# Linear attention as one pipeline over units of two tile pairs, with its weights built in an earlier stage

## The chip, the cores and the metric

The kernel runs on one core of one Trainium2 chip. The metric is the device time of the whole program in microseconds, as the median over several runs. The kernel is one program of about 4.3 ms in which nine stages follow each other; the change is inside one of them and touches one other.

## The reference, cut to what matters

The input X has 2 x 1024 rows of 128 values. Two local stacks of six layers each make up most of the time; between them stands a linear attention over the pairs of rows (0, n) and (1, n), so the sequence has two positions:

```python
qn = _ln(query, g1, b1)                    # query = layernorm(x)
q = relu(_phm(qn, qA, qS, qb))
k = relu(_phm(query, kA, kS, kb))
v = _phm(query, vA, vS, vb)
idx = np.pi / 2 * jnp.arange(1, L + 1)[None, :, None] / L      # L = 2 positions, 16 heads of 8
q_, k_ = concat([q * s, q * c]), concat([k * s, k * c])        # s, c = sin(idx), cos(idx)
attn = (q_ @ (k_.T @ v)) / max(q_ . sum(k_), 1e-6)
out = _ln(attn + qn, g2, b2)
x = x + _phm(out, oA, oS, ob) + out
```

`_phm(x, A, S, b)` is x @ W + b, where the 128x128 matrix W is a sum of four Kronecker products of a 4x4 with a 32x32 matrix.

## The kernel before

X lies in SBUF as 16 tiles of 128 rows by 128 columns; `NT` is 16, `TB` is 8 tiles of each position, and `NG` is 4 groups of four tiles. PS is the PSUM memory of eight banks of 512 columns. The names of the engines in the code are `te` (TensorE, PE in the profile), `ve` (VectorE, DVE), `ac` (ScalarE, ACT), `gp` (GpSimd, POOL) and `sp` (SyncE). The order on each engine is the order in which the code writes it; no scheduler changes it. Engines wait for each other's semaphores. `then` makes VectorE wait for its own last instruction, and `fence()` is a barrier of all engines that also clears the semaphores.

`linear_attention` has three passes with a barrier behind each. The first builds the four weights on VectorE (L1124, L1126), and then, group by group, takes statistics (L201, L205, L208), lets POOL take the root (L212), normalises on VectorE (L221), turns on TensorE (L237), copies on ScalarE (L1098), multiplies by the weights of K and V (L1115), and adds the bias on VectorE out of PSUM (L1105, L1138). The second does the same for Q with gain and shift (L227, L229), and behind its last group VectorE alone does the attention for all tiles (`dve_attend`, L1174 to L1188). The third normalises the result, multiplies by the last weight (L1205) and adds to X (L1216 to L1219). Statistics of the next group run ahead, but the wait on `kv_mm`, `lq_mm` or `lo_mm` stands in VectorE's order before the next group's normalisation:

```python
if g < NG - 1:
    norm_stats(g + 1, X)
norm_apply(g, X, group(XN, g))
ve.wait_ge(kv_mm, g + 1)
```

In `cope_attention`, an earlier stage of the same form, POOL only takes the roots of four groups and adds a bias behind the next barrier (L1055).

## Time and profile before

| what | us |
|---|---|
| median of 3 runs | 4346.16 (4344.17 to 4351.9) |
| the profiled execution | 4355.26, of which the span is 4354.0 |
| linear attention, from first to last instruction of VectorE | 2488.55 to 2634.38 |
| first local stack | 778.83 to 2487.48 |
| second local stack, with the output's transfer | 2635.45 to 4353.9 |

The rows of the profile are of one execution. Busy times are the sums of an engine's instructions in a stretch. The granted clock is a share of TensorE's full 2.4 GHz, so 0.50 is 1.2 GHz. A tensor multiplication in f32 appears as two matmul records of PE.

### The profile page before, as it was taken

The page shows a single profiled execution, that of the slowest core. Times are in us where ns is not written, and L with a number is a line of the kernel's source. Part 1 is how long each engine was busy: PE and PEld are TensorE (multiplying, and loading weights), DVE is VectorE, ACT ScalarE, POOL GpSimd, SP SyncE. Part 2 cuts the span into 40 slices and gives each one's busy share as a digit, 9 for nine tenths or more (in the row PEclk, how much of TensorE's full clock was granted, in tenths as well). Part 3 has the DMA queues.
Part 4 walks back from the last instruction along what each step waited for, and adds up shares of the span by engine and source line. Part 5 has one row for each costly group of instructions (what it writes and reads, how often), then busy time and mean ns, then how long its engine had stood idle before and what let it go on. Part 6 is the DMA issues. An engine that isn't in the chain of part 4 may idle for free. (4 is left out here: it accounts for less than half of the span.)

```text
span 4354.0 us, 158762 instructions
## 1 busy us (share of the span) xinstructions
PE 3861.5 (89%) x66864; PEld 2706.7 (62%) x66864; DVE 3055.7 (70%) x6301; ACT 2565.4 (59%) x4921; POOL 2642.3 (61%) x2220
## 2 busy tenths in 40 slices
PE   7988792799999999999999536999999999999996
PEld 5655561466666766667666424666666676666764
DVE  4456576777777778777787357778777777877773
ACT  3335360466767666666676304666666666766764
POOL 2039092676676767667676206766666677767772
PEclk7569896899999999999999757999999999999998
DMA  3000000132333323333333101333333233333222
GB/s 97 1 1 1 1 1 0 43 95 65 93 80 77 88 72 87 82 82 82 77 86 84 38 0 41 87 76 86 78 84 80 74 88 84 78 80 80 67 71 55
DMA packets 303234, 276.83 MB, mean 64 GB/s; under 512 B 158136, under 2 KB 201664, under 8 KB 302528
## 3 DMA queue, kind: packets, MB, share of 16 engines
q1 hardware_dynamic: 302528, 266.68, 24.1%
q8 instruction: 533, 8.73, 0.9%
q14 instruction: 173, 1.42, 0.1%
HBM read 51.58 MB, written 1.05 MB: 12 GB/s over the span
## 5 line engine op out<-in xcount | busy, mean ns | idle before, releaser
L1350 PE MATMUL PS<-l_wqkv,XNT 128*128 128x512 f32 x768 | 392.1, 633 | 0.6 <-issue 0.4
L1344 PE MATMUL PS<-l_wqkv,XNT 128*128 128x512 f32 x768 | 381.1, 619 | 2.5 <-issue 1.5
L1337 PE MATMUL PS<-l_wqkv,XNT 128*128 128x512 f32 x768 | 368.8, 603 | 6.1 <-DVE l_UQ L1619 2.3
L1492 ACT ACTIVATE m_sq<-PS 128x512 f32<-128x512 f32 x384 | 225.9, 595 | 197.4 <-PE PS L1344 160.6
L1492 ACT ACTIVATE l_sq<-PS 128x512 f32<-128x512 f32 x384 | 226.0, 595 | 197.3 <-PE PS L1344 160.4
L1758 POOL TENSOR_TENSOR l_Pm<-l_Pm,l_rs 128x1024 f32<-128x1024 f32 x96 | 182.8, 1904 | 237.1 <-DVE l_rs L1629 237.1
L1758 POOL TENSOR_TENSOR m_Pm<-m_Pm,m_rs 128x1024 f32<-128x1024 f32 x96 | 182.8, 1904 | 233.2 <-DVE m_rs L1629 233.2
L1647 DVE TENSOR_TENSOR XN<-PS,XN 128x128 f32<-128x128 f32 x192 | 56.1, 292 | 281.4 <-PE PS L1396 281.4
L1616 DVE TENSOR_TENSOR l_QR<-PS,l_rot 128x512 f32<-128x512 f32 x192 | 131.7, 686 | 164.8 <-ACT l_sq L1492 158.5
L1616 DVE TENSOR_TENSOR m_QR<-PS,l_rot 128x512 f32<-128x512 f32 x192 | 131.7, 686 | 164.2 <-ACT m_sq L1492 158.0
L1753 POOL TENSOR_TENSOR m_QR<-m_QR,m_UQ 128x1024 f32<-128x1024 f32 x96 | 227.7, 2372 | 19.8 <-DVE m_UQ L1619 19.8
L1753 POOL TENSOR_TENSOR l_QR<-l_QR,l_UQ 128x1024 f32<-128x1024 f32 x96 | 227.7, 2372 | 19.5 <-DVE l_UQ L1619 19.5
L212 POOL TENSOR_TENSOR rstd<-rstd,minus_half 128x4 f32<-128x4 f32 x40 | 41.7, 1044 | 307.2 <-DVE rstd L208 307.2
L1753 POOL TENSOR_TENSOR m_KR<-m_KR,m_UK 128x1024 f32<-128x1024 f32 x96 | 226.8, 2363 | 0.2 <-DVE m_UK L1619 0.2
L1753 POOL TENSOR_TENSOR l_KR<-l_KR,l_UK 128x1024 f32<-128x1024 f32 x96 | 226.7, 2362 | 0.2 <-DVE l_UK L1619 0.2
L1634 DVE TENSOR_REDUCE l_sums<-l_sq 128x16 f32<-128x1024 f32 x192 | 219.1, 1182 | 0.0
L1634 DVE TENSOR_REDUCE m_sums<-m_sq 128x16 f32<-128x1024 f32 x192 | 219.1, 1182 | 0.0
L1366 PEld LDWEIGHTS PS<-m_V,m_pT 64*32 64x32 f32 x12288 | 131.6, 106 | 126.6 <-issue 66.5
L1366 PEld LDWEIGHTS PS<-l_V,l_pT 64*32 64x32 f32 x12288 | 132.2, 106 | 123.2 <-issue 70.8
L1350 PEld LDWEIGHTS PS<-l_wqkv,XNT 128*128 128x128 f32 x768 | 133.5, 194 | 116.8 <-issue 100.0
L1344 PEld LDWEIGHTS PS<-l_wqkv,XNT 128*128 128x128 f32 x768 | 130.9, 190 | 115.6 <-issue 96.1
L1366 PE MATMUL PS<-m_V,m_pT 64*32 64x64 f32 x12288 | 153.1, 227 | 49.4 <-DMA m_V<-m_Vt 35.5
(363 smaller groups left out, 11342.7 us busy)
## 6 DMA issues: line engine op xcount, KB each, us to landing
l_V<-l_Vt SPq DMA_DIRECT2D x576, 128.0 KB
m_V<-m_Vt SPq DMA_DIRECT2D x576, 128.0 KB
l_V<-l_Vt SPq DMA_DIRECT2D x384, 64.0 KB
m_V<-m_Vt SPq DMA_DIRECT2D x384, 64.0 KB
l_wqkv<-l_wqkv_dram SPq DMA_DIRECT2D x144, 128.0 KB, 2.4
l_rot<-l_rot_dram SPq DMA_DIRECT2D x48, 256.0 KB, 3.9
l_wo<-l_wo_dram SPq DMA_DIRECT2D x24, 256.0 KB, 3.5
l_w<-l_w_dram SPq DMA_DIRECT2D x12, 341.0 KB
```

What stands on the lines that cost most here:

```text
L212: gp.tensor_tensor(rstd[:, g % 2, :], rstd[:, g % 2, :], minus_half[:, 0:4], ALU.pow).then_inc(rstd_out)
L1337: te.matmul(PS[:, b, :], tile_T(n), weights(n, b * 512, (b + 1) * 512), start=True, stop=True).then_inc(q_pr)
L1344: te.matmul(PS[:, 2 + b, :], tile_T(n), weights(n, INNER + b * 512, INNER + (b + 1) * 512), start=True, stop=True).then_inc(k_pr)
L1350: m = te.matmul(PS[:, r, :], tile_T(n), wv, start=True, stop=True)
L1366: m = te.matmul(PS[LW * w:LW * (w + 1), 6 + r, c * LD:(c + 1) * LD], pT[64 * r:64 * r + 64, c, LW * w:LW * (w + 1)], V2[64 * r:64 * r + 64 ...
L1492: ac.activation(sq[:, c, b * 512:(b + 1) * 512], PS[:, 2 * c + b, :], ACT.Square).then_inc(sq_out)
L1616: ve.tensor_tensor(R[:, n % 2, heads, :], src, over(rot[:, par, 2 * c, i, :], 1, [P, 8, LD]), ALU.mult)
L1634: ve.tensor_reduce(sums2[:, c * LH:(c + 1) * LH, 0], sq[:, c, :].rearrange("p (h d) -> p h d", d=LD), AX, ALU.add).then_inc(ssr_out)
L1647: ve.tensor_tensor(Y[:, i, :], PS[:, 5, 0:D], Y[:, i, :], ALU.add).then_inc(y_add)
L1753: gp.tensor_tensor(R[:, n % 2, :, :], R[:, n % 2, :, :], U[:, :, :], ALU.add).then_inc((aq_out, ak_out)[c])
L1758: gp.tensor_tensor(pm, pm, over(rs[:, :], 2, [P, 16, 2 * LW]), ALU.mult).then_inc(pn_out)
```

## The change

The weights of the linear attention are built on POOL in the cope stage, behind its four roots, and kept in `d_w`. `linear_attention` is written anew. A unit `u` is two tiles of position 0 and the same two of position 1 (`tile`), so that a unit has all that its attention needs. In each of seven rounds every engine does what is due for different units: in round r keys, values and queries of unit r, attention of unit r - 1, second norm of unit r - 2, output of unit r - 3. There is one barrier, at the end. Statistics of all 16 tiles are taken at once; the norm of the norm is not measured but computed from the first variance (`root2`). ScalarE normalises (activation with scale and bias) and takes K, Q and V out of PSUM; TensorE adds the bias by a product of a row of ones with the bias row into the same bank (`projected`); POOL adds shifts and gains and sums the normalised result into X. What is removed are the three passes printed above. The diff, with declarations left out:

```diff
@@ -98,7 +98,7 @@
-        d_fact, d_blocks = sb("d_fact", P, 4, 4, 4), sb("d_blocks", P, 4, 4, D // 4)
+        d_w = sb("d_w", P, 4, D)
...
+        d_fact, d_blocks, d_part = se("d_fact", P, 4, 4, 4), se("d_blocks", P, 4, 4, D // 4), se("d_part", P, 2, D)
@@ -1021,6 +1022,16 @@
                 def pool():
                     for g in range(NG):
                         norm_root(g)
+                    shape = [P, 4, D // 4]
+                    for m4 in range(4):
+                        whole = d_w[:, m4, :].rearrange("p (j l) -> p j l", j=4)
+                        for k in range(4):
+                            to = whole if k == 0 else d_part[:, k % 2, :].rearrange("p (j l) -> p j l", j=4)
+                            G.step(gp.tensor_tensor(to, over(d_fact[:, m4, k, :], 2, shape), over(d_blocks[:, m4, k, :], 1, shape), ALU.mult))
+                            G.wait()
+                            if k:
+                                G.step(gp.tensor_tensor(whole, whole, to, ALU.add))
+                                G.wait()
@@ -1068,160 +1079,233 @@
...
         def linear_attention():
...
+                wq, wk, wv, wo = (d_w[:, m4, :] for m4 in range(4))
                 g1, b1, g2, b2 = (d_gain[:, k, :] for k in range(4))
...
+                U = [P, NG, 4, D]
+                xn, qn, k4, v4, q4 = (sl(n, *U) for n in ("xn", "QN", "k", "v", "q"))
...
+                xT, qT, aT = (sl(n, P, 4 * P) for n in ("xT", "qT", "aT"))
...
+                def tile(u, j):
+                    return TB * (j // 2) + 2 * u + j % 2
+                def unit(src, u):
+                    return src[:, :, :].rearrange("p (s i) d -> p s i d", s=2)[:, :, 2 * u:2 * u + 2, :]
...
+                def pe():
+                    def turned(bank, src):
                         for j in range(4):
+                            m = te.transpose(PS[:, bank, j * P:(j + 1) * P], src[:, j, :], ident[:, :])
+                        return m
+                    def projected(bank, m4, lhs, w):
+                        te.matmul(PS[:, bank, :], ones[0:1, :], over(d_bias[0:1, m4, :], 1, [1, 4, D]), start=True, stop=False, skip_group_check=True)
                         for j in range(4):
+                            m = te.matmul(PS[:, bank, j * D:(j + 1) * D], lhs[:, j * P:(j + 1) * P], w, start=False, stop=True, skip_group_check=True)
+                        return m
+                    te.wait_ge(dready, 1)
+                    for r in range(NG + 3):
+                        if r < NG:
+                            te.wait_ge(dxn_out, r + 1)
+                            if r:
+                                te.wait_ge(dxT_out, r)
+                            turned(0, xn[:, r, :, :]).then_inc(dxT_mm)
+                            te.wait_ge(dxT_out, r + 1)
+                            if r:
+                                te.wait_ge(dk_out, r)
+                                te.wait_ge(dv_out, r)
+                            projected(1, 1, xT, wk)
+                            projected(2, 2, xT, wv).then_inc(dkv_mm)
+                            te.wait_ge(dqn_out, r + 1)
+                            if r:
+                                te.wait_ge(dqT_out, r)
+                            turned(3, qn[:, r, :, :]).then_inc(dqT_mm)
+                            te.wait_ge(dqT_out, r + 1)
+                            if r:
+                                te.wait_ge(dq_out, r)
+                            projected(4, 0, qT, wq).then_inc(dq_mm)
+                        u = r - 3
+                        if u >= 0:
+                            te.wait_ge(daff_out, u + 1)
+                            if u:
+                                te.wait_ge(daT_out, u)
+                            turned(5, an[:, u, :, :]).then_inc(daT_mm)
+                            te.wait_ge(daT_out, u + 1)
+                            if u:
+                                te.wait_ge(dx_out, u)
+                            projected(6, 3, aT, wo).then_inc(do_mm)
+                def act():
+                    for r in range(NG + 3):
+                        if r < NG:
+                            ac.wait_ge(dshift_out, 1)
+                            for j in range(4):
+                                n = tile(r, j)
+                                m = ac.activation(xn[:, r, j, :], X[:, n, :], ACT.Identity, scale=root[:, n:n + 1], bias=shift[:, n:n + 1])
+                            m.then_inc(dxn_out)
+                            ac.wait_ge(dxT_mm, r + 1)
+                            if r:
+                                ac.wait_ge(dkv_mm, r)
+                            ac.copy(xT[:, :], PS[:, 0, :]).then_inc(dxT_out)
+                            ac.wait_ge(dkv_mm, r + 1)
+                            ac.activation(k4[:, r, :, :].rearrange("p j d -> p (j d)"), PS[:, 1, :], ACT.Relu).then_inc(dk_out)
+                            ac.copy(v4[:, r, :, :].rearrange("p j d -> p (j d)"), PS[:, 2, :]).then_inc(dv_out)
+                            ac.wait_ge(dqT_mm, r + 1)
+                            if r:
+                                ac.wait_ge(dq_mm, r)
+                            ac.copy(qT[:, :], PS[:, 3, :]).then_inc(dqT_out)
+                            ac.wait_ge(dq_mm, r + 1)
+                            ac.activation(q4[:, r, :, :].rearrange("p j d -> p (j d)"), PS[:, 4, :], ACT.Relu).then_inc(dq_out)
+                        u = r - 2
+                        if 0 <= u < NG:
+                            ac.wait_ge(dashift_out, u + 1)
+                            for j in range(4):
+                                m = ac.activation(an[:, u, j, :], att[:, u, j, :], ACT.Identity, scale=aroot[:, u % 2, j:j + 1], bias=ashift[:, u % 2, j:j + 1])
+                            m.then_inc(dan_out)
+                        u = r - 3
+                        if u >= 0:
+                            ac.wait_ge(daT_mm, u + 1)
+                            if u:
+                                ac.wait_ge(do_mm, u)
+                            ac.copy(aT[:, :], PS[:, 5, :]).then_inc(daT_out)
+                def dve():
+                    def attend(u):
+                        ve.wait_ge(dk_out, u + 1)
+                        ve.wait_ge(dv_out, u + 1)
+                        ve.wait_ge(dq_out, u + 1)
+                        V.wait()
+                        for s in range(2):
+                            q = q4[:, u, 2 * s:2 * s + 2, :].rearrange("p i d -> p (i d)")
+                            m = ve.tensor_tensor(prod[:, s, :, :], k4[:, u, :, :].rearrange("p (k i) d -> p k (i d)", k=2), over(q, 1, [P, 2, 2 * D]), ALU.mult)
+                        then(m)
+                        then(ve.tensor_reduce(dots[:, :, :, :].rearrange("p s k h -> p (s k h)"),
+                                              prod[:, :, :, :].rearrange("p s k (h d) -> p (s k h) d", d=DH), AX, ALU.add))
+                        then(ve.tensor_tensor(dots[:, :, :, :], dots[:, :, :, :], turn[:, :, :, 0:2, :].rearrange("p s k i h -> p s k (i h)"), ALU.mult))
+                        then(ve.tensor_tensor(den[:, :, :], dots[:, :, 0, :], dots[:, :, 1, :], ALU.add))
+                        then(ve.tensor_scalar(den[:, :, :], den[:, :, :], 1e-6, None, ALU.max))
+                        then(ve.reciprocal(den[:, :, :], den[:, :, :]))
+                        then(ve.tensor_tensor(dots[:, :, :, :], dots[:, :, :, :], over(den[:, :, :], 2, [P, 2, 2, 2 * H]), ALU.mult))
+                        for s in range(2):
+                            weight = over(dots[:, s, :, :].rearrange("p k h -> p (k h)"), 2, [P, 4 * H, DH])
+                            m = ve.tensor_tensor(prod[:, s, :, :].rearrange("p k (h d) -> p (k h) d", d=DH),
+                                                 v4[:, u, :, :].rearrange("p j (h d) -> p (j h) d", d=DH), weight, ALU.mult)
+                        then(m)
+                        a = att[:, u, :, :].rearrange("p (s i) d -> p s (i d)", s=2)
+                        then(ve.tensor_tensor(a, prod[:, :, 0, :], prod[:, :, 1, :], ALU.add))
+                        then(ve.tensor_tensor(att[:, u, :, :], att[:, u, :, :], qn[:, u, :, :], ALU.add))
+                    def measure(u):
+                        par = u % 2
+                        if u >= 2:
+                            ve.wait_ge(dan_out, u - 1)
+                        for j in range(4):
+                            m = ve.bn_stats(ast[:, par, j, :], att[:, u, j, :])
+                        then(m)
+                        for j in range(4):
+                            m = ve.bn_aggr(amv[:, par, j, :], ast[:, par, j, :])
+                        then(m)
+                        ve.tensor_scalar(aroot[:, par, :], amv[:, par, :, 1], EPS, None, ALU.add).then_inc(davar_out)
+                    for n in range(NT):
+                        m = ve.bn_stats(st[:, n, :], X[:, n, :])
+                    then(m)
+                    for n in range(NT):
+                        m = ve.bn_aggr(mv[:, n, :], st[:, n, :])
+                    then(m)
+                    ve.tensor_scalar(root[:, :], mv[:, :, 1], EPS, None, ALU.add).then_inc(dvar_out)
+                    ve.wait_ge(droot_out, 1)
+                    ve.scalar_tensor_tensor(shift[:, :], mv[:, :, 0], -1.0, root[:, :], ALU.mult, ALU.mult).then_inc(dshift_out)
+                    then(ve.tensor_tensor(root2[:, :], mv[:, :, 1], root[:, :], ALU.mult))
+                    then(ve.tensor_tensor(root2[:, :], root2[:, :], root[:, :], ALU.mult))
+                    ve.tensor_scalar(root2[:, :], root2[:, :], EPS, None, ALU.add).then_inc(dvar2_out)
+                    ve.wait_ge(droot2_out, 1)
+                    ve.wait_ge(dready, 1)
+                    for r in range(NG + 4):
+                        if r < NG:
+                            ve.wait_ge(dxn_out, r + 1)
+                            for j in range(4):
+                                n = tile(r, j)
+                                m = ve.scalar_tensor_tensor(qn[:, r, j, :], xn[:, r, j, :], root2[:, n:n + 1], g1, ALU.mult, ALU.mult)
+                            m.then_inc(dqg_out)
+                        u = r - 2
+                        if 0 <= u < NG:
+                            ve.wait_ge(daroot_out, u + 1)
+                            ve.scalar_tensor_tensor(ashift[:, u % 2, :], amv[:, u % 2, :, 0], -1.0, aroot[:, u % 2, :], ALU.mult, ALU.mult).then_inc(dashift_out)
+                        u = r - 1
+                        if 0 <= u < NG:
+                            attend(u)
+                            measure(u)
+                        u = r - 4
+                        if u >= 0:
+                            ve.wait_ge(do_mm, u + 1)
+                            ve.wait_ge(dres_out, u + 1)
+                            ve.tensor_tensor(unit(X, u), PS[:, 6, :].rearrange("p (s i d) -> p s i d", s=2, i=2), unit(X, u), ALU.add).then_inc(dx_out)
+                def pool():
...
+                    G.wait()
+                    gp.memset(ones[:, :], 1.0).then_inc(dready)
+                    gp.wait_ge(dvar_out, 1)
+                    gp.tensor_tensor(root[:, :], root[:, :], minus_half[:, 0:NT], ALU.pow).then_inc(droot_out)
+                    gp.wait_ge(dvar2_out, 1)
+                    gp.tensor_tensor(root2[:, :], root2[:, :], minus_half[:, 0:NT], ALU.pow).then_inc(droot2_out)
+                    for r in range(NG + 3):
+                        if r < NG:
+                            gp.wait_ge(dqg_out, r + 1)
+                            gp.tensor_tensor(qn[:, r, :, :], qn[:, r, :, :], over(b1, 1, [P, 4, D]), ALU.add).then_inc(dqn_out)
+                        u = r - 2
+                        if 0 <= u < NG:
+                            gp.wait_ge(dan_out, u + 1)
+                            G.step(gp.tensor_tensor(an[:, u, :, :], an[:, u, :, :], over(g2, 1, [P, 4, D]), ALU.mult))
+                            G.wait()
+                            gp.tensor_tensor(an[:, u, :, :], an[:, u, :, :], over(b2, 1, [P, 4, D]), ALU.add).then_inc(daff_out)
+                            gp.wait_ge(daff_out, u + 1)
+                            gp.tensor_tensor(unit(X, u), unit(X, u), pairs(an[:, u, :, :]), ALU.add).then_inc(dres_out)
+                        u = r - 1
+                        if 0 <= u < NG:
+                            gp.wait_ge(davar_out, u + 1)
+                            gp.tensor_tensor(aroot[:, u % 2, :], aroot[:, u % 2, :], minus_half[:, 0:4], ALU.pow).then_inc(daroot_out)
+                pe()
+                act()
+                dve()
+                pool()
                 fence()
```

The order on the engines follows. On TensorE, where the names before the arrow are the target bank and behind it weights and moving data, the stage began with a turn and key and value products and had these rows at the start of the first and the second pass:

```order
L237 MATMUL PS<-ident,XN 128x128 x4
L1115 MATMUL PS<-d_wk,xT 128x128
L1115 MATMUL PS<-d_wv,xT 128x128
...
L237 MATMUL PS<-ident,d_QN 128x128 x4
L1153 MATMUL PS<-d_wq,xT 128x128 x4
```

It now has this in round 3, the first in which all parts are present:

```order
L1128 MATMUL PS<-ident,d_xn 128x128 x4
L1132 MATMUL PS<-d_bias,d_ones 128x512
L1134 MATMUL PS<-d_w,d_xT 128x128 x4
L1132 MATMUL PS<-d_bias,d_ones 128x512
L1134 MATMUL PS<-d_w,d_xT 128x128 x4
L1128 MATMUL PS<-ident,d_QN 128x128 x4
L1132 MATMUL PS<-d_bias,d_ones 128x512
L1134 MATMUL PS<-d_w,d_qT 128x128 x4
L1128 MATMUL PS<-ident,d_an 128x128 x4
L1132 MATMUL PS<-d_bias,d_ones 128x512
L1134 MATMUL PS<-d_w,d_aT 128x128 x4
```

Keys, values, queries and output of different units now stand behind each other, each with a bias product of 512 columns ahead of it.

On ScalarE the whole stage was twelve copies between the last layer before and the table load of the next stack:

```order
L1547 ACTIVATE xT<-PS,l_b 128x512 x2
L1547 ACTIVATE xT<-PS,l_b 85x512
L1098 COPY xT<-PS 128x512 x12
L1549 ACT_TABLE_LOAD
L1526 COPY XNT<-PS 64x512
```

Now rounds 2 and 3 read so on ScalarE:

```order
L1175 ACTIVATE d_xn<-X,d_shift,d_root 128x128 x4
L1180 COPY d_xT<-PS 128x512
L1182 ACTIVATE d_k<-PS 128x512
L1183 COPY d_v<-PS 128x512
L1187 COPY d_qT<-PS 128x512
L1189 ACTIVATE d_q<-PS 128x512
L1194 ACTIVATE d_an<-d_att,d_ashift,d_aroot 128x128 x4
L1175 ACTIVATE d_xn<-X,d_shift,d_root 128x128 x4
L1180 COPY d_xT<-PS 128x512
```

The normalisation of the next round stands behind the last evacuation of this one and, from round 2 on, behind that of a result.

On POOL the stage had four roots in each pass, with the barriers (L120) between:

```order
L120 ISA
L212 TENSOR_TENSOR rstd<-rstd,minus_half 128x4 x4
L120 ISA
L212 TENSOR_TENSOR rstd<-rstd,minus_half 128x4 x4
L120 ISA
```

Now, from the stage's begin to its first sum into X:

```order
L1281 MEMSET d_turn 128x128 x4
L1283 MEMSET d_ones 128x128
L1285 TENSOR_TENSOR d_root<-d_root,minus_half 128x16
L1287 TENSOR_TENSOR d_root<-d_root,minus_half 128x16
L1291 TENSOR_TENSOR d_QN<-d_QN,d_gain 128x512 x2
L1303 TENSOR_TENSOR d_aroot<-d_aroot,minus_half 128x4
L1291 TENSOR_TENSOR d_QN<-d_QN,d_gain 128x512
L1295 TENSOR_TENSOR d_an<-d_an,d_gain 128x512
L1297 TENSOR_TENSOR d_an<-d_an,d_gain 128x512
L1299 TENSOR_TENSOR X<-X,d_an 128x2x256
L1303 TENSOR_TENSOR d_aroot<-d_aroot,minus_half 128x4
```

Behind the three operations of a unit (L1295, L1297, L1299) stands the root of the unit after it (L1303).

## Rows read from the trace of the kernel before

**Rows 1.** The page, its head.
```profile
span 4354.0 us, 158762 instructions
```

**Rows 2.** Order of time on VectorE: start, length, instruction, idle before it and its releaser.
```profile
2488.55 0.29 DVE L1124 TENSOR_TENSOR d_wq<-d_fact,d_blocks 128x128 f32<-128x128 f32 x1 [1.07 <-PEq L120]
...
2497.68 0.87 DVE L201 BATCH_NORM_STATS2 stats<-X 128x6 f32<-128x128 f32 x4
...
2633.69 0.69 DVE L1219 TENSOR_TENSOR X<-PS,X 128x512 f32<-128x512 f32 x1 [2.58 <-PE PS L1205]
2635.45 0.87 DVE L201 BATCH_NORM_STATS2 stats<-X 128x6 f32<-128x128 f32 x4 [1.06 <-PEq L120]
```

**Rows 3.** Stretches: PE, PEld, DVE, ACT, POOL busy (count), clock, DMA share, GB/s.
```profile
2538.21:2599.88 61.67, 12.77 (x48) 9.99 (x48) 43.11 (x93) 2.34 (x4) 4.17 (x4) 0.51 0.00 0
...
2488.55:2635.45 146.90, 45.13 (x176) 36.80 (x176) 91.05 (x257) 7.06 (x13) 12.55 (x13) 0.51 0.00 0
```

**Rows 4.** Order of time on all engines: the first group's keys and values.
```profile
2501.64 1.12 PE L237 MATMUL PS<-ident,XN 128*128 128x128 f32 x4 [15.61 <-DVE XN L221]
2502.80 0.58 ACT L1098 COPY xT<-PS 128x512 f32<-128x512 f32 x1 [20.55 <-PE PS L237]
...
2503.43 0.80 PE L1115 MATMUL PS<-d_wk,xT 128*128 128x128 f32 x2 [0.68 <-ACT xT L1098]
...
2506.58 0.63 PE L1115 MATMUL PS<-d_wv,xT 128*128 128x128 f32 x2
2507.26 0.69 DVE L1105 TENSOR_TENSOR d_kv<-PS,d_bias 128x512 f32<-128x512 f32 x1 [5.67 <-PE PS L1115]
```

**Rows 5.** Groups of instructions in the stage: count, busy us, mean ns, idle before.
```profile
L1176 DVE TENSOR_REDUCE d_dots<-d_prod 128x128 f32<-128x1024 f32 x4 | 4.9, 1220 | 0.1
...
L205 DVE BATCH_NORM_AGGREGATE meanvar<-stats 128x2 f32<-128x6 f32 x48 | 4.5, 157 | 0.4
...
L201 DVE BATCH_NORM_STATS2 stats<-X 128x6 f32<-128x128 f32 x16 | 3.5, 277 | 0.0
...
L1216 DVE TENSOR_TENSOR X<-X,xn 128x512 f32<-128x512 f32 x4 | 2.8, 691 | 0.1
...
L1180 DVE RECIPROCAL d_den<-d_den 128x256 f32<-128x256 f32 x1 | 1.8, 1753 | 0.0
```

**Rows 6.** Groups on POOL by form, 665 to 830 us.
```profile
L212 POOL TENSOR_TENSOR rstd<-rstd,minus_half 128x4 f32<-128x4 f32 x8 | 8.3, 1044 | 27.9 <-DVE rstd L208 27.9
...
L1055 POOL TENSOR_TENSOR X<-X,c_bo 128x512 f32<-128x512 f32 x4 | 4.9, 1266 | 65.3 <-SPq L120 65.3
...
L748 POOL TENSOR_TENSOR X<-X,g_y 128x128 f32<-128x128 f32 x2 | 0.9, 452 | 0.2
```

**Rows 7.** Order of time on ScalarE: normalising four tiles by scale and bias.
```profile
2470.97 1.65 ACT L1533 ACTIVATE xn<-l_xsh,l_fmid,l_frs 128x128 f32<-128x128 f32 x4 [16.94 <-DVE l_fmid L1667]
```

**Rows 8.** Order of time on TensorE, second stack's begin: two 512-column products.
```profile
2655.50 1.96 PE L1337 MATMUL PS<-l_wqkv,XNT 128*128 128x512 f32 x4 [2.21 <-DVE m_UQ L1619]
```

**Rows 9.** Order of time on TensorE in the cope stage.
```profile
679.53 5.49 PE L953 MATMUL PS<-c_w,xT 128*128 128x384 f32 x8 [0.68 <-ACT xT L961]
689.29 1.12 PE L237 MATMUL PS<-ident,xn 128*128 128x128 f32 x4 [4.28 <-DVE xn L221]
```

**Rows 10.** Stretches, columns as in rows 3.
```profile
685.00:687.00 2.00, 0.01 (x1) 0.00 (x0) 1.95 (x3) 0.00 (x0) 0.00 (x0) 0.84 0.00 0
689.00:691.00 2.00, 1.12 (x4) 0.72 (x4) 0.23 (x1) 0.56 (x1) 0.33 (x1) 0.51 0.00 0
...
2654.00:2656.50 2.50, 1.00 (x3) 0.55 (x4) 2.50 (x7) 0.00 (x0) 1.07 (x1) 1.00 0.00 0
...
80.00:240.00 160.00, 159.33 (x1154) 104.88 (x1153) 64.64 (x95) 55.61 (x95) 13.19 (x9) 0.50 0.00 1
```

**Rows 11.** One line of VectorE in the mixture stage: min, median, max ns.
```profile
L707 DVE TENSOR_TENSOR g_y<-g_y,g_x x16: 1225/1562/3390, 544.2 to 665.7; 128x1024 f32<-128x1024 f32 x16
```

More of the change, by code:

```diff
@@ L1091, in then @@
                     V.wait()
-                def turn_copies(mm):
-                    for g in range(NG):
-                        ac.wait_ge(turn_mm, g + 1)
-                        if g >= 2:
-                            ac.wait_ge(mm, g - 1)
-                        ac.copy(xT4[:, g % 2, :], PS[:, 7 * (g % 2), :]).then_inc(xT_out)
-                def roots():
-                    for g in range(NG):
-                        norm_root(g)
-                def biased(to, bank_cols, bias, out_sem):
-                    ve.tensor_tensor(to, bank_cols, over(bias, 1, [P, 4, D]), ALU.add).then_inc(out_sem)
@@ L1156, in dve_queries @@
-                def dve_queries():
-                    norm_stats(0, XN)
-                    for g in range(NG):
-                        if g < NG - 1:
-                            norm_stats(g + 1, XN)
-                        norm_apply(g, XN, group(QN, g), affine=(g1, b1))
-                        ve.wait_ge(lq_mm, g + 1)
-                        biased(group(q, g), PS[:, 1:5, 0:D], bs["q"][:, :], lq_out)
-                        ve.wait_ge(lq_out, g + 1)
-                        V.step(ve.tensor_scalar(group(q, g), group(q, g), 0.0, None, ALU.max))
@@ L1178, in dve_attend @@
-                    then(ve.tensor_tensor(den[:, :, :], dots[:, :, 0, :], dots[:, :, 1, :], ALU.add))
-                    then(ve.tensor_scalar(den[:, :, :], den[:, :, :], 1e-6, None, ALU.max))
-                    then(ve.reciprocal(den[:, :, :], den[:, :, :]))
-                    then(ve.tensor_tensor(dots[:, :, :, :], dots[:, :, :, :], over(den[:, :, :], 2, [P, 2, 2, P]), ALU.mult))
-                    for s in range(2):
-                        for k, to in ((0, prod), (1, prod2)):
-                            a = over(heads(dots[:, s, k, :]), 3, full)
-                            m = ve.tensor_tensor(split(to[:, :, :]), split(kv[:, TB * k:TB * (k + 1), D:]), a, ALU.mult)
-                        then(m)
-                        then(ve.tensor_tensor(prod[:, :, :], prod[:, :, :], prod2[:, :, :], ALU.add))
-                        then(ve.tensor_tensor(att[:, TB * s:TB * (s + 1), :], prod[:, :, :], QN[:, TB * s:TB * (s + 1), :], ALU.add))
@@ L1208, in dve_out @@
-                def dve_out():
-                    norm_stats(0, att)
-                    for g in range(NG):
-                        par, xg = g % 2, group(X, g)
-                        if g < NG - 1:
-                            norm_stats(g + 1, att)
-                        norm_apply(g, att, xn4[:, par, :, :], affine=(g2, b2))
-                        ve.wait_ge(xn_out, g + 1)
-                        then(ve.tensor_tensor(xg, xg, xn4[:, par, :, :], ALU.add))
-                        then(ve.tensor_tensor(xg, xg, over(bs["o"][:, :], 1, [P, 4, D]), ALU.add))
-                        ve.wait_ge(lo_mm, g + 1)
-                        ve.tensor_tensor(xg, PS[:, 1 + par, :].rearrange("p (j d) -> p j d", j=4), xg, ALU.add).then_inc(lo_out)
```

100 lines of the change are left out of this document (18 added, 82 removed).

## The prediction

> **What bounds the kernel now.** I read the page first (its span [rows 1]), then the stretches of the linear attention, then the order of time on VectorE, on TensorE and on ScalarE there. The stage lasts from VectorE's first weight product at 2488.55 to the first statistics of the next stack at 2635.45 [rows 2], 146.9 us of 4354.0. Nothing of another stage runs inside it: a barrier stands at both ends and two stand within. In these 146.9 us VectorE works 91.1, TensorE 45.1, POOL 12.6, ScalarE 7.1, and TensorE's granted clock is 0.51, the lower of its two levels of 1.2 and 2.4 GHz [rows 3]. The reader is to see that no engine is full. The engines work one after another, as one group of keys and values shows: VectorE normalises, TensorE turns (1.12), ScalarE copies (0.58), TensorE multiplies (2503.43 to 2507.2), and VectorE, which has waited 5.67 us, takes the result out [rows 4]. In the stretch that holds the query pass and the attention VectorE is busy 43.1 of 61.7 [rows 3]. So the stage is a chain, and its length is the sum of VectorE's work and of what VectorE waits for.
>
> **What the change removes.** The 28 weight products and sums leave VectorE; between the row at 2488.55 and the first statistics at 2497.68 they fill 9.1 us, 28 at 0.326 [rows 2]. Two barriers go, each 1.1 us as the idle time before the row at 2635.45 shows [rows 2]. Statistics of the second norm go, since it is now computed from the first. What remains is a new order of work, so I don't subtract: I build the new stage's length from its chain and set it against 146.9.
>
> **Head.** Sixteen statistics at 4 in 0.87 are 3.5 us, sixteen aggregations at 94 ns are 1.5, one scalar and the handoffs 0.3: 5.3 [rows 5]. Then POOL takes a power of 16 columns. The trace has only 4 columns, at 1.04 [rows 6]. Bounds: 1.0 if the cost is fixed, 4.2 if it is all by column. Plain POOL work grows with its elements (128 columns 0.45, 512 columns 1.27, [rows 6]), so about 0.2 is fixed and 4 columns of power cost 0.8: I take 3.4. With the shift, 0.3, the first normalisation on ScalarE starts at 9.0. The second power is beside ScalarE's and TensorE's first work and costs nothing here; it has some 4 us of cover before TensorE asks for the query's norm.
>
> **A round.** In each of four rounds ScalarE and TensorE hand one unit to and fro, and neither has another unit to work on: ScalarE's next normalisation stands behind its last copy of this round. The steps, with handoffs: normalise, 4 in 1.65 [rows 7]; turn, 1.15 at the low clock as in [rows 4], 0.65 at the high one; copy 0.65; keys and values; their two evacuations 1.25 (TensorE turns the queries beside them); copy 0.65; query product; evacuation 0.65. A 128-column product costs 0.427 at the low clock (eight in 3.8 less 0.35 of latency, [rows 4]), so the new 512-column bias product costs 1.71, as much as four of them: the bias is no longer added on VectorE but doubles TensorE's work. Keys and values are 2 x 1.71 + 8 x 0.427 + 0.35 = 7.2 low; the high clock halves all but the latency, 3.8, and two 512-column products in 1.96 at the high clock agree with that [rows 8]. The query product is 3.8 or 2.1. A round is 17.0 at the low clock and 11.4 at the high one. From the third round on ScalarE also normalises an attention result, 1.7.
>
> **Which clock.** In the cope stage a stretch of 5.49 us from 679.53 brought the clock up as it ended (0.84 between 685 and 687), and an idle of 4.28 us behind it lost it again, 0.51 between 689 and 691 [rows 9, 10]. An idle of 2.21 us in the next stack did not lose it (1.00, [rows 8, 10]). Here keys and values run 7.2 us at the low clock, longer than that stretch, so it rises within them; I take it after 4.5 us, and the product ends at 5.9. That makes round 0 14.0. Between the query product and the next turn lie 0.65 + 1.65 = 2.3 us, close to the gap that kept it: rounds 1 and 2 get 11.9, the high value with 0.5 for a partial loss. With ScalarE's extra 1.7 the gap is 4.0, close to the one that lost it, so round 3 starts low, 14.0. Round 3 begins at 9.0 + 14.0 + 11.9 + 11.9 + 1.7 = 48.5.
>
> **Tail**, counted from there. POOL gives unit 0 its gain, its shift and its sum into X, three 128x512 operations at 1.27 to 1.3 [rows 6] (3.9), and only behind them in its order stands unit 1's root (1.1); VectorE's shift for unit 1 follows at 5.2. Attend for unit 2: two products 1.3, reduction 1.26, five operations of 64 or 128 columns 1.7, of which I put the reciprocal of 64 columns at 0.55 (1.75 for 256, [rows 5]), two weightings 1.3, two sums 1.4 (512 columns in 0.69, [rows 5]), in all 7.0 and 0.1 for handoffs, 7.1; statistics 1.5. ScalarE's last copy of round 3 is at 14.0, unit 1's normalisation ends at 15.7, POOL's three operations at 19.6, the root of unit 2 at 20.7, the shift at 20.9. Here VectorE waits for POOL. Attend for unit 3 with what POOL costs it (next paragraph), 9.6, ends at 30.5, its statistics at 32.0, the sum of unit 0 into X, 0.7, at 32.7. Behind that sum TensorE can do the outputs of units 1, 2 and 3: product 3.0, then twice turn, copy and product 4.5 (5.6 low, 3.4 high, I take the middle), 44.7, last sum 45.4. The stage is 48.5 + 45.4 + barrier 1.1 = 95.0 against 146.9: 51.9 saved.
>
> **POOL beside VectorE.** A VectorE sum of 1,024 columns whose operands both lie in SBUF takes 1.22 at least and up to 3.39 in the mixture stage, where POOL is busy; the median of 16 is 1.57 [rows 11]. Six of Attend's operations have such operands, and POOL's three for unit 2 fall into Attend for unit 3. Bounds: nothing, or all of POOL's 3.8; I take 2.5, and 0.8 in Attend for unit 2, which is off the chain. The Trainium skill, "SBUF — State Buffer", Who interferes with whom, says that such a VectorE instruction and a POOL instruction that reads SBUF contend, and that the second blocks wholly until the first ends; by that rule the term is 3.8 and the time 1.3 us more. It speaks against handing POOL this work, and the trace agrees with the direction.
>
> **Weights in the cope stage.** POOL's last root there is over before VectorE's attention begins, and it then idles 65.3 us until the sums of L1055 [rows 6]. The 28 operations at 0.45 are 12.6 us and fit. Cost 0; if VectorE had to give way for all of them, 12.6.
>
> **The rivals.** (a) As summed, own range 4287 to 4301, 0.50. (b) The clock falls in every round, because the turns at a round's start don't hold it: rounds 1 and 2 cost 14.0, +4.2, 4298; 0.15. For it: the cope stage's turns at 689.29 ran low [rows 9]; against it the 2.21 us gap. The Trainium skill, "TensorE: Matmul & The Clock Gate", Part 4, says that a transpose doesn't count as busy work for the clock in the way a product does; by it the turns here would hold nothing and the time is 4298, where the sum has 4294. (c) The clock stays low throughout as before: 9.0 + 3 x 17.0 + 1.7, tail 51.4 by the same steps, 114.2 with the barrier, 32.7 saved, 4313; 0.08. Against it: a stretch of 7.2 us is longer than any that the stage has now. (d) High throughout: 85.7, 61.2 saved, 4285; 0.15. (e) VectorE gives way to the weights in the cope stage: 4294 + 12.6 = 4307; 0.05. (f) Slower: the next stack, on which TensorE is nearly full, meets the state of 80 to 240 us, where TensorE was busy 159.3 of 160 and yet got 0.50 [rows 10]. Each us of its work then takes two, so 104 us at the low clock eat the 52 saved, and a hold of 160 us gives +80, 4374. Nothing in the diff touches that stack; 0.05. (g) The gain is eaten by something unseen and nothing changes, 4346; 0.02.
>
> **How the numbers follow.** The profiled run took 4355.3, its span 4354.0; 4355.3 - 51.9 = 4303.4. It lay 9.1 above the median of the runs, 4346.2, so the forecast for the median is 4294. The range reaches down to (d) with a power of 1.0 (2.4 less), 4283, and a little contention less, 4281; upward past (b) and (e) towards (c), to 4309, which leaves out about half of (c) and the slow cases, together some 0.15. About 0.2%, 8.7 us, is what a measurement of this kernel can tell from no change. Faster 0.93, same 0.02, slower 0.05.
>
> **What would show it.** One barrier pair around a stage of about 94 us with no idle between passes; sixteen-column powers on POOL of 3 to 4 us; keys and values in about 6 us, then under 4; VectorE waiting for POOL's root before Attend of units 2 and 3; 28 POOL operations in the cope stage and no longer VectorE rows there. I am wrong if ScalarE stalls between units (its order shows no table load there), if the clock never rises, or if Attend is much over 8 us.

## The result and the profile after

The changed kernel takes 4313.73 us (median of 4 runs, 4304.96 to 4314.31). The kernel before took 4345.16 on the same chip. The ratio is 0.9923, interval [0.9908, 0.9938]: 31.4 us are saved where 52 were forecast, and the median lies above the forecast range of 4281 to 4309. The profiled execution took 4313.86, its span 4312.6.

The stage, in VectorE's order of time in the changed kernel, from its first to the first row of the next stack; between them the two waits to look at:

```profile
2492.85 3.19 DVE L1242 BATCH_NORM_STATS2 d_st<-X 128x6 f32<-128x128 f32 x16 [1.18 <-PEq L121]
...
2578.36 0.16 DVE L1265 SCALAR_TENSOR_TENSOR d_ashift<-d_amv,d_aroot 128x4 f32<-128x4 f32 x1 [9.59 <-POOL d_aroot L1303]
...
2594.32 0.69 DVE L1274 TENSOR_TENSOR X<-PS,X 128x512 f32<-128x512 f32 x1 [3.54 <-PE PS L1134]
...
2603.25 0.87 DVE L202 BATCH_NORM_STATS2 stats<-X 128x6 f32<-128x128 f32 x4 [1.18 <-PEq L121]
```

It lasts 110.4 us against the 146.9 of [rows 2, 3] and the 95.0 of the sum. The same kernel by stretches, columns as in [rows 3]: the stage, then its head, its three first rounds and the rest, the cope stage, and the second stack.

```profile
2492.85:2603.25 110.40, 70.16 (x208) 41.88 (x208) 50.76 (x145) 25.72 (x57) 32.91 (x28) 0.55 0.00 0
...
2492.85:2500.68 7.83, 0.00 (x0) 0.00 (x0) 4.74 (x35) 0.01 (x1) 3.71 (x6) 0.53 0.00 1
2500.68:2516.70 16.02, 12.23 (x38) 7.28 (x38) 1.53 (x7) 4.28 (x9) 4.16 (x2) 0.59 0.00 1
2516.70:2534.52 17.82, 14.13 (x38) 8.29 (x38) 9.21 (x25) 4.28 (x11) 3.27 (x2) 0.51 0.00 0
2534.52:2553.88 19.36, 14.13 (x38) 8.30 (x38) 9.29 (x26) 5.82 (x15) 2.32 (x1) 0.50 0.00 0
2553.88:2603.25 49.37, 29.67 (x94) 18.00 (x94) 25.98 (x53) 11.34 (x27) 19.45 (x17) 0.57 0.00 0
...
672.59:781.66 109.07, 36.38 (x96) 22.75 (x96) 63.67 (x103) 7.26 (x12) 20.92 (x37) 0.56 0.00 0
...
2603.25:4312.60 1709.35, 1606.12 (x31584) 1131.97 (x31584) 1266.62 (x2528) 1132.68 (x2112) 1160.13 (x984) 0.98 0.30 77
```

The same two stretches of the kernel before, not shown until now:

```profile
673.76:778.83 105.07, 33.32 (x96) 19.71 (x96) 62.94 (x104) 7.26 (x12) 9.17 (x9) 0.60 0.00 0
...
2635.45:4354.00 1718.55, 1610.60 (x31584) 1134.45 (x31584) 1263.99 (x2528) 1133.82 (x2112) 1159.98 (x984) 0.98 0.30 77
```

The spans differ by 41.4: 36.5 is the stage; 9.2 is the second stack, which has the same instructions and was merely longer in that execution of before; the cope stage gives back 4.0; the start and the first stack make up the rest. Whole executions scatter by about 10 us in this way, so the stage's length in the traces says more about the change than one total does.

The stage is 15.4 us longer than the sum, and 13.7 of this lie in the first three rounds. The head is 7.8 (forecast 9.0), the three rounds 53.2 (14.0 + 11.9 + 13.6 = 39.5), the rest with its barrier 49.4 (46.5). Round 3, with which the rest begins, missed in the same way: ScalarE's last evacuation in it ended 17.9 us after its begin, where the forecast had 14.0. In rounds 1 and 2 TensorE is busy 14.1 of 17.8 and 19.4 at a clock of 0.51 and 0.50. The first round and the begin of the next in order of time on TensorE, in the changed kernel:

```profile
2504.23 2.07 PE L1132 MATMUL PS<-d_bias,d_ones 1*128 1x512 f32 x2 [0.67 <-ACT d_xT L1180]
2506.23 2.08 PE L1134 MATMUL PS<-d_w,d_xT 128*128 128x128 f32 x8
2508.23 2.07 PE L1132 MATMUL PS<-d_bias,d_ones 1*128 1x512 f32 x2
2510.23 2.08 PE L1134 MATMUL PS<-d_w,d_xT 128*128 128x128 f32 x8
...
2513.96 1.12 PE L1132 MATMUL PS<-d_bias,d_ones 1*128 1x512 f32 x2 [0.80 <-ACT d_qT L1187]
...
2518.39 1.11 PE L1128 MATMUL PS<-ident,d_xn 128*128 128x128 f32 x4 [2.22 <-ACT d_xn L1175]
```

Three things are to be seen. Keys and values run 7.87 us without a gap, and the last product (2.08) is as slow as the first: the clock has not risen within them, only behind them, ahead of the query's bias (1.12); the granted clock is 0.50 up to 2513.1 and 1.00 from 2514 on. It is 0.50 again from 2517.4 on, within the pause of 2.22 us, and the next turn is slow (1.11). And a product begins 2.00 us behind the one before it, where four 128-column products should take 1.71.

### The profile page after: what moved, and what is told of

Its sections match the earlier page's. It is cut to its first block and busy times, and to the rows that moved or that the text cites. A ratio compares the mean times of both kernels' runs of the same rounds, so it can differ in the third digit from the quotient of the medians.

```text
span 4312.6 us, 158783 instructions
## 1 busy us (share of the span) xinstructions
PE 3882.3 (90%) x66896; PEld 2713.4 (63%) x66896; DVE 3020.3 (70%) x6190; ACT 2583.8 (60%) x4965; POOL 2674.5 (62%) x2263
## 3 DMA queue, kind: packets, MB, share of 16 engines
HBM read 51.58 MB, written 1.05 MB: 12 GB/s over the span
## 5 line engine op out<-in xcount | busy, mean ns | idle before, releaser
L1434 PEld LDWEIGHTS PS<-l_wqkv,XNT 128*128 128x128 f32 x768 | 132.3, 192 | 114.8 <-issue 98.0
L1428 PEld LDWEIGHTS PS<-l_wqkv,XNT 128*128 128x128 f32 x768 | 131.0, 190 | 114.7 <-issue 95.1
L1421 PEld LDWEIGHTS PS<-l_wqkv,XNT 128*128 128x128 f32 x768 | 132.8, 193 | 102.1 <-issue 102.1
L1450 PE MATMUL PS<-l_V,l_pT 64*32 64x64 f32 x12288 | 153.8, 228 | 45.1 <-DMA l_V<-l_Vt 31.4
```

The costliest lines, as they stand in the source:

```text
L1421: te.matmul(PS[:, b, :], tile_T(n), weights(n, b * 512, (b + 1) * 512), start=True, stop=True).then_inc(q_pr)
L1428: te.matmul(PS[:, 2 + b, :], tile_T(n), weights(n, INNER + b * 512, INNER + (b + 1) * 512), start=True, stop=True).then_inc(k_pr)
L1434: m = te.matmul(PS[:, r, :], tile_T(n), wv, start=True, stop=True)
L1450: m = te.matmul(PS[LW * w:LW * (w + 1), 6 + r, c * LD:(c + 1) * LD], pT[64 * r:64 * r + 64, c, LW * w:LW * (w + 1)], V2[64 * r:64 * r + 64 ...
```

## The experiments

In all of them the stage is measured as above, from VectorE's first statistics to those of the next stack, in the one execution of each kernel that was profiled. The ratio intervals of the change, e2 and e3 overlap, and so do those of e1, e5, e6 and e7: within these two groups the totals can't tell the kernels apart, and what is said of them goes by the stage.

| kernel | median, us | before, same chip | ratio, interval | stage, us |
|---|---|---|---|---|
| the change | 4313.73 | 4345.16 | 0.9923 [0.9908, 0.9938] | 110.40 |
| e1_rows128 | 4297.87 | 4354.24 | 0.9868 [0.9852, 0.9884] | 97.09 |
| e2_rows32 | 4319.01 | 4354.24 | 0.9917 [0.9903, 0.9932] | 106.77 |
| e3_rows64 | 4319.75 | 4354.24 | 0.9918 [0.9901, 0.9934] | 113.75 |
| e4_nobias | 4290.3 | 4354.24 | 0.985 [0.9835, 0.9865] | 81.72 |
| e5_early | 4307.77 | 4363.73 | 0.9871 [0.9844, 0.9897] | 90.00 |
| e6_rows128_early | 4302.16 | 4363.73 | 0.9848 [0.9823, 0.9874] | 83.47 |
| e7_rows128_tail | 4309.26 | 4363.73 | 0.987 [0.9843, 0.9897] | 94.04 |
| e8_weights_only | 4349.36 | 4363.73 | 0.9969 [0.9953, 0.9986] | 137.53 |
| b1_all | 4290.97 | 4357.21 | 0.9843 [0.9825, 0.9861] | 77.74 |
| b2_root_first | 4290.02 | 4357.21 | 0.9851 [0.9825, 0.9876] | 77.19 |

**e1_rows128.** The bias product gets 128 rows of weights 1/128 (the bias tile already holds the bias in every row). The result, the columns and the number of instructions stay.

```diff
-te.matmul(PS[:, bank, :], ones[0:1, :], over(d_bias[0:1, m4, :], 1, [1, 4, D]), ...)
+te.matmul(PS[:, bank, :], ones[0:128, :], over(d_bias[0:128, m4, :], 1, [128, 4, D]), ...)
-gp.memset(ones[:, :], 1.0)
+gp.memset(ones[:, :], 1.0 / 128)
```

> The bias product uses all 128 rows (weights of 1/128, the bias row repeated on all partitions) in place of one row; its 512 columns stay. Theory A, the clock takes a product that uses one row for almost no activity: now the clock rises within the keys-and-values stretch of every round, the stage falls from 110.4 us to 92 to 98, and the 0.29 us that each change between one-row and full products costs (28 changes, 8 us, inside this figure) are gone. Theory B, the pauses of 2 us and more between the rounds hold the clock down whatever the product: granted clock stays at 0.50 to 0.55 and the stage only loses the changes, 102 to 106 us. Median of the runs: A 4293 to 4300, B about 4306.

The same rows of TensorE in this kernel:

```profile
2503.89 2.08 PE L1132 MATMUL PS<-d_bias,d_ones 128*128 128x512 f32 x2 [0.68 <-ACT d_xT L1180]
2505.76 1.92 PE L1134 MATMUL PS<-d_w,d_xT 128*128 128x128 f32 x8
2507.47 1.91 PE L1132 MATMUL PS<-d_bias,d_ones 128*128 128x512 f32 x2
2509.18 1.29 PE L1134 MATMUL PS<-d_w,d_xT 128*128 128x128 f32 x8
2510.30 0.60 PE L1128 MATMUL PS<-ident,d_QN 128*128 128x128 f32 x4
...
2516.36 1.05 PE L1128 MATMUL PS<-ident,d_xn 128*128 128x128 f32 x4 [2.23 <-ACT d_xn L1175]
```

The clock now rises within keys and values, as the prediction had it, in this and in each later round, and the products follow each other at 1.71. ScalarE's normalisations stand at 2500.33, 2514.67, 2528.60 and 2543.97: rounds of 14.3, 13.9 and 15.4 where the changed kernel has 16.0, 17.8 and 19.4. The stage is 97.1, where the prediction's sum had 95.0. What still fails is the pause: the granted clock is 1.00 through its 2.23 us and falls as the next turn begins, which takes 1.05. Ahead of round 3 it outlasts even 3.78 us and the turn (0.66), and falls as keys and values begin:

```profile
2545.67 0.66 PE L1128 MATMUL PS<-ident,d_xn 128*128 128x128 f32 x4 [3.78 <-ACT d_xn L1175]
2547.01 1.93 PE L1132 MATMUL PS<-d_bias,d_ones 128*128 128x512 f32 x2 [0.68 <-ACT d_xT L1180]
```

**e2_rows32 and e3_rows64.** The same edit with 32 rows of 1/32 and with 64 rows of 1/64.

> The bias product uses 32 rows (weights 1/32). Theory A with activity by rows used: too little, clock low as with one row, stage 108 to 112 us. Theory B: the same stage as with one row. If the clock rises here as with 128 rows, it is not the count of rows but something of the single row.

> The bias product uses 64 rows (weights 1/64). Theory A by rows used: between the two, the clock rises in some of the rounds, stage 95 to 110 us. Theory B: no difference from one row, 110 us.

With 64 rows, on TensorE:

```profile
2505.74 2.07 PE L1132 MATMUL PS<-d_bias,d_ones 64*128 64x512 f32 x2 [0.68 <-ACT d_xT L1180]
2507.74 2.07 PE L1134 MATMUL PS<-d_w,d_xT 128*128 128x128 f32 x8
2509.74 2.07 PE L1132 MATMUL PS<-d_bias,d_ones 64*128 64x512 f32 x2
2511.74 2.08 PE L1134 MATMUL PS<-d_w,d_xT 128*128 128x128 f32 x8
```

Neither the late clock nor the 2.00 us is gone; both come as with one row. With 1, 32 and 64 rows the clock rose within keys and values in none of the twelve rounds; with 128 it did in all eight of e1 and e7. In the 64-row kernel the pause ahead of round 1 did not cost the clock, which fell only behind the turn:

```profile
2519.91 0.66 PE L1128 MATMUL PS<-ident,d_xn 128*128 128x128 f32 x4 [2.23 <-ACT d_xn L1175]
```

Both stages miss what was expected, e2 by 1.2 us below 108 to 112 and e3 by 3.8 us above 95 to 110. The stages of 106.8, 110.4 and 113.8 with 32, 1 and 64 rows are not in the order of the rows; they differ by where the clock happened to rise for a while. Among the row counts tried only the full 128 behaves otherwise. Whether the clock answers to the rows or to the 0.29 us that TensorE loses at each change of rows no run tells apart, since the two came and went together.

**e4_nobias.** It leaves the biases out of the four projections, so its output lacks them.

> Leaves the sixteen bias products out, so K, Q, V and the output lack their biases; all else as in the changed kernel. It prices what adding the bias on TensorE costs. TensorE's keys and values are then eight products, 3.8 us at the low clock, 8.0 before; the queries 2.1 in place of 4.3. Both theories: a round falls from 17.8 to about 11.5, the stage to 78 to 84 us. Theory A also says that full products with no weak ones between may bring the clock up in some rounds; theory B says it stays at 0.50.

```profile
2494.02:2575.74 81.72, 38.28 (x176) 32.61 (x176) 51.78 (x146) 25.84 (x57) 32.97 (x28) 0.60 0.00 1
```

TensorE is busy 38.3 us instead of 70.2, and the stage is 28.7 us shorter: that is the whole price of the bias products where they stand in the changed kernel. The clock stays at 0.60 in the mean, hardly above the 0.55 with them; e1, with as many columns as the changed kernel, has 0.72. All products here have 128 rows, and yet the query products of rounds 0 and 3 still run at the low clock (2.08 us each): full rows alone don't bring it up.

**e5_early and e6_rows128_early.** ScalarE normalises the next unit right behind its copy of xT, while TensorE multiplies keys and values; e5 with one row, e6 with 128.

```diff
 ac.copy(xT[:, :], PS[:, 0, :]).then_inc(dxT_out)
+if r + 1 < NG:
+    normal(r + 1)        # the four activations that stood at the head of round r + 1
 ac.wait_ge(dkv_mm, r + 1)
```

> One-row bias products as in the changed kernel; ScalarE normalises the next unit right behind its copy of this one, while TensorE multiplies, and no longer behind the last evacuation. The pause of TensorE before a turn falls from 2.2 us to about 0.6. The gap theory (the pauses hold the clock down) expects the clock to rise now: stage 95 us or less. The row theory expects it to stay at 0.50 apart from chance rises, and the stage to lose only 3 x 1.65 us of the chain: 104 to 107 us.

> Both: 128-row bias products and the early normalisation. Row theory: the clock rises in the first round and, with pauses of 0.6 us, is kept through the rounds, so a round is at most 10 to 11 us and VectorE's 11 us of a unit become the limit: stage 82 to 88 us. If the pauses did not matter for keeping it, only 5 us come off the 97.1 of the 128-row kernel: 92 us.

On TensorE in e5, from the first query product on:

```profile
2519.88 1.12 PE L1132 MATMUL PS<-d_bias,d_ones 1*128 1x512 f32 x2 [0.80 <-ACT d_qT L1192]
2520.93 1.16 PE L1134 MATMUL PS<-d_w,d_qT 128*128 128x128 f32 x8
2521.93 0.60 PE L1128 MATMUL PS<-ident,d_xn 128*128 128x128 f32 x4
...
2525.39 1.22 PE L1132 MATMUL PS<-d_bias,d_ones 1*128 1x512 f32 x2
2526.54 2.07 PE L1134 MATMUL PS<-d_w,d_xT 128*128 128x128 f32 x8
```

Without the pause the clock passes from round 0 into round 1 (0.60 for the turn). Then it falls, and the product at 2526.54 takes 2.07, in the midst of gapless keys and values, one-row products among them. So with one-row products the clock neither comes up in time nor stays. But the stage of 90.00 is what the gap theory expected (95 or less) and far below the 104 to 107 of the row theory: the mean clock of the stage is 0.67 where the changed kernel has 0.55, and taking out the pauses alone gave more (20.4 us) than filling the rows alone (13.3). Both matter here. With 128 rows and no pause it holds; in e6:

```profile
2525.00:2552.00 27.00, 19.54 (x110) 13.86 (x110) 22.10 (x51) 12.17 (x27) 6.69 (x6) 1.00 0.00 0
```

The stage of e6 is 13.6 us shorter than that of e1, and that of e5 20.4 shorter than the changed kernel's. The edit also takes 1.65 us of normalising and the handoffs out of rounds 1 to 3, some 5 us, so these sums aren't the clock's alone.

**e7_rows128_tail.** e1 with VectorE's sum of unit r-4 into X ahead of the attention of unit r-1.

> The 128-row kernel with VectorE's sum into X of unit r - 4 written ahead of the attention of unit r - 1 instead of behind it, so that the output product of unit 1 need not wait 13.5 us for the attention of unit 3. If the tail is TensorE's row of three output products behind that sum, the stage loses 2 to 5 us of 97.1. If the tail is the way of unit 3 itself (root, shift, normalisation, POOL's gain and shift, turn, product), it loses under 1 us.

94.04 against 97.09. In the changed kernel the bias product for the output of unit 1 waits for that sum until 2590.24, 11.46 us; the tail is held up by an order of two VectorE steps. By the totals e7 and e1 can't be told apart.

**e8_weights_only.** The kernel before with nothing but the weights moved to POOL in the cope stage.

> The kernel before with one part of the change alone: the weights are built on POOL in the cope stage; the three passes of the linear attention are as before. The stage should fall by the 9.1 us of the 28 operations, 146.9 to 137.8, and the cope stage stay as long as it was; median 9 us under the kernel before. If VectorE gave way to POOL in the cope stage, that stage grows by up to 12.6 us and nothing is won.

Its stage is 137.53, 9.4 less than before; the prediction had 9.1 for the 28 operations. Its cope stage lasts 105.37 against 105.07. In the changed kernel the 28 operations stand on POOL without a gap (16 of the first line's kind, 12 of the second's):

```profile
712.32 0.40 POOL L1030 TENSOR_TENSOR d_part<-d_fact,d_blocks 128x128 f32<-128x128 f32 x1
712.80 0.45 POOL L1033 TENSOR_TENSOR d_w<-d_w,d_part 128x128 f32<-128x128 f32 x1
```

Beside them VectorE's normalisations took 385 ns each instead of 343, and the stage grew by 0.3 us, so they cost next to nothing. The 4.0 us of the changed kernel's cope stage are not theirs: its last products ran at the low clock. One of them, in the changed kernel and in the kernel before in turn:

```profile
770.47 2.08 PE L1054 MATMUL PS<-c_wo,xT 128*128 128x128 f32 x8 [0.68 <-ACT xT L1062]
```

```profile
771.34 1.16 PE L1043 MATMUL PS<-c_wo,xT 128*128 128x128 f32 x8 [0.68 <-ACT xT L1051]
```

TensorE's work ahead of them is the same, and all of it has 128 rows; in the ten further kernels with the weights on POOL the cope stage took 105.4 to 109.1 us. What decides it there was not tried.

**b1_all and b2_root_first.** All edits that helped in one kernel, the bias products ahead of the waits for the transposed copy, and the next unit's turn ahead of the output of an earlier one; then the same with POOL's root of unit 3 ahead of its three operations for unit 2.

```diff
...
+bias(4, 0)                      # was the first line of projected, behind the wait
 te.wait_ge(dqT_out, r + 1)
+product(4, qT, wq).then_inc(dq_mm)
...
```

> Four edits together: the bias product with 128 rows of weights 1/128; ScalarE normalises the next unit right after it has copied xT out; TensorE issues the bias products ahead of the wait for the transposed copy, and turns the next unit ahead of the output of an earlier one; VectorE adds the output of unit r-4 to X before the attention of unit r-1. The first two gave a stage of 83.47 us together. The theory that TensorE's own products still set the length of a round expects the stage to be shorter by the bias products that leave the path (1.0 to 2.0 us a round with three of them, so 3 to 6 us) and by the 3.05 us that the last edit gave by itself: 74 to 78 us, and a ratio near 0.983. The rival, that VectorE's 11 us a unit already set the rounds, expects the hoisted products to buy nothing and the last edit alone 3 us: 80 us.

> The same kernel, and in the fourth turn of GpSimd's loop (r = 4, unit 3) the inverse root of unit 3's variances is taken ahead of the three operations of unit 2 on an and X, so that these run after the attention of unit 3 and not beside it. If those three operations are what makes the attention of unit 3 last 9.42 us in place of 7.05, it falls to about 7.05 here, and VectorE doesn't wait for the root. Against it the output of unit 2 comes some 6 us later, and the two last outputs follow each other at 4.5 us. Expected: attention 7.05 us, the stage between 2 us shorter and 3 us longer than without the change. The rival, that the attention of unit 3 is slow for another reason (the activation's reads or the product's), leaves 9.4 us.

b1's stage is 77.74, ratio 0.9843: 5.7 us under e6's, of which e7's edit had given 3.05 on top of e1. If the gains add, some 2.7 are left for the bias products ahead of the waits and the new place of the turn. It is faster than the kernel before, and its interval lies below the changed kernel's. In b2 the attention of unit 3 lasts 7.08 us (2554.21 to 2561.29); in b1 9.11 (2548.88 to 2557.99), in the changed kernel 9.46 (2578.54 to 2588.00). The stage gained only 0.5 over b1, since from the end of that attention to the stage's end it now takes 1.9 us more. Operations of that attention on VectorE, in the changed kernel for unit 2 and then for unit 3:

```profile
2563.10 0.22 DVE L1216 TENSOR_TENSOR d_den<-d_dots 128x64 f32<-128x64 f32 x1
2563.36 0.20 DVE L1217 TENSOR_SCALAR d_den<-d_den 128x64 f32<-128x64 f32 x1
...
2581.73 1.24 DVE L1216 TENSOR_TENSOR d_den<-d_dots 128x64 f32<-128x64 f32 x1
2583.00 1.27 DVE L1217 TENSOR_SCALAR d_den<-d_den 128x64 f32<-128x64 f32 x1
2584.31 0.55 DVE L1218 RECIPROCAL d_den<-d_den 128x64 f32<-128x64 f32 x1
```

and POOL beside the latter:

```profile
2581.62 1.26 POOL L1297 TENSOR_TENSOR d_an<-d_an,d_gain 128x512 f32<-128x512 f32 x1
2582.96 1.26 POOL L1299 TENSOR_TENSOR X<-X,d_an 128x512 f32<-128x512 f32 x1
```

VectorE's operations of 0.2 us now end at 2582.97 and 2584.27, where POOL's operations end (2582.88 and 2584.22). The reciprocal begins behind them, with POOL idle, and takes 0.55 as for unit 2. The price is 2.4 us, and b2 takes it away by moving POOL's three operations alone. This agrees with the Trainium skill, "SBUF — State Buffer", Who interferes with whom, by which a VectorE instruction with two SBUF inputs, or a tensor_scalar in a two-port mode, that meets a POOL instruction reading SBUF waits until that one has ended. Whether the tensor_scalar here is in such a mode no row shows. The term stays under the 3.8 us of all three POOL operations, since each VectorE operation waited only for what was left of one.

## Why the prediction was wrong

The direction was right, the size was not. The step that failed is in **Which clock**: "Here keys and values run 7.2 us at the low clock, longer than that stretch, so it rises within them". It didn't: keys and values of round 0 took 8.1 us where 5.9 were taken, and those of rounds 1 and 2 as much where 3.8 were. The stretch in [rows 9] consisted of full products. Here half of the time belonged to one-row products, and e1 shows that the clock rises within keys and values with 128 rows and not with one, at equal columns and without gaps in both. The 4.5 us after which it was taken to rise come from no row shown: the 5.49 us of [rows 9] passed wholly at 0.50, and in e1 the rise came 3.6 to 5.8 us after the start. The prediction also had a row that showed a busy TensorE to be not enough: in [rows 10] it was busy 159.3 of 160 us and got 0.50. It was used for the rival of a slower next stack (f), and its cause was not looked for. TensorE's three costliest groups in that stretch of the kernel before:

```profile
L338 PE MATMUL PS<-ident,a_S 128*128 128x128 f32 x177 | 48.1, 427 | 0.7 <-DVE X L485 0.7
L348 PE MATMUL PS<-a_vc,a_pT 128*64 128x9 f32 x704 | 45.4, 258 | 0.0
L325 PE MATMUL PS<-a_kTm,a_qT 32*64 32x512 f32 x168 | 41.7, 1084 | 0.0
```

48.1 us are transposes, 45.4 are products of 9 columns, 41.7 are products of 32 rows. After e1 to e3 the last line may be part of the cause; no run here changed that stage, so it isn't shown, and neither of the other two is ruled out. Rival (c), low throughout, comes nearest to what came: the clock was high only for the query product of round 0 and at the stage's end. That its 4313 is the measured time is luck: its stage of 114.2 is 3.8 us too long, and the cope stage, which it left alone, was 4.0 longer in the profiled execution.

The second failed assumption is that a pause of 2.3 us keeps the clock. [rows 8, 10] show one of 2.21 that did; behind the pauses of 2.22 and 2.23 ahead of rounds 1 and 2 in the changed kernel and in e1 the clock was low. Even with a full bias product it was thus rival (b) whose times held: rounds of 14.3, 13.9 and 15.4 in e1, where (b) has 14.0, 14.0 and 15.7. Its reason, that turns don't hold the clock, wasn't tested. Between the changed kernel and e1 lie 13.3 us, the rise of the clock and the dearer changes between kinds of products together. No run parts them. By the rows, four changes in each of four rounds and one in each of four outputs run without a gap, 20 at 0.29 at most, so an estimate is up to 5.8 us for the changes and at least 7.5 for the clock.

Point by point. **Head**: the power of 16 columns took 2.90 where 3.4 was taken, the sixteen statistics 3.19 for 3.5 and the sixteen aggregations 1.17 for 1.5:

```profile
2497.53 2.90 POOL L1285 TENSOR_TENSOR d_root<-d_root,minus_half 128x16 f32<-128x16 f32 x1 [3.82 <-DVE d_root L1247]
```

**A round**: the step list and its order were right; "keys and values 7.2" is mis-sized, 8.1 with the latency at the end, and the query product 4.1 for 3.8, as each change of kind costs 0.29. That makes the low round 17.8 for 17.0. "As much as four of them" for the bias product was right, and it is the dearest item of the change, 28.7 us by e4. **Tail**: 48.2 for 45.4, at a low clock for most of it, round 3 above all; VectorE waits for POOL's root ahead of the attention of unit 3, as said. **POOL beside VectorE**: 2.4 for 2.5, in the place that was named, and nothing for the 0.8 in the attention of unit 2 (7.08). **Weights**: next to nothing, as said, and 9.4 for 9.1 saved. **The median**: the profiled run lay 9.1 above it, and its second stack was 9.2 longer than in the changed kernel's trace, so this was likely that stack's scatter. **The slower rival** (f) didn't come: the second stack has a clock of 0.98 as before.

## What to carry to other kernels

A bias added by a product of one row costs TensorE as many columns as the product that it corrects and can hold the clock of a sparsely used TensorE low; in such a stage fill the rows (128 rows of 1/128 gave 13 us here), issue it before the wait (at most 2.7 here), or try the bias on another engine, which no run did here (without it the stage is 28.7 shorter). Where an engine pair hands one unit to and fro, order the next unit's first step behind the last copy that it needs, not behind the round: this took out the pause that lost the clock, and 20.4 us of the stage with one row, 13.6 with 128. When a view shows an engine that is full and yet slow, as [rows 10] did, find what its instructions have in common before the forecast rests on a rise of the clock.

## What was not expected of the hardware

Beside products of 1, 32 or 64 rows the granted clock did not rise over up to 7.9 us without a gap, in twelve rounds of three kernels, where 128 rows brought it up 3.6 to 5.8 us after their start in each round of e1; in e5 the clock fell in the midst of gapless work. The changeover between a product with fewer than 128 rows and one with 128 took 0.29 us more than between two full ones at the low clock (2.00 against 1.71), with 1, 32 and 64 rows alike. A pause of 2.2 us lost the clock in the changed kernel and kept it in [rows 8] and in e3; in e1 one of 3.78 kept it. What decides, no run shows: a pause's length alone doesn't.
